# Key-on-partition scores of a causal attention: where the two mask products of a half stand among its score products

## The reference

```python
x = x + attn_a(layernorm(x)); x = x + ffn(layernorm(x))
x = x + attn_b(layernorm(x)); x = x + ffn(layernorm(x))
# attn_a:
S = einsum('hid,hjd->hij', K, Q) * HEAD_DIM ** -0.5
S = where(delta < 0, -inf, S) + decay       # delta = i - j, decay = -|delta|
attn = einsum('hij,hjd->hid', softmax(S), V) @ o_w.T + o_b
# attn_b: scores = q k / sqrt(16), where(causal, scores, -inf), softmax, times v, @ Wo + bo
# ffn: two shared experts, and 32 routed ones of which each token takes 6
```

## Time and profile before

| | |
|---|---|
| median of 3 runs | 3063.31 us (3061.61 to 3063.41) |
| span of the profiled execution | 3108.0 us |
| PE busy in that span | 2643.3 us (85%) |
| DVE / ACT / POOL busy | 2095.1 / 1642.7 / 1403.2 us |
| stretches of attention | about 153 to 846 us and 1700 to 2384 us |
| products at L1607 / masks at L1611 | 1536 / 1024 |

### The profile page before, as it was taken

How to read it: one execution, slowest core, us unless ns; L and a number is a source line. 1 busy time by engine, 2 the same in 40 slices (tenths; PEclk the granted TensorE clock), 3 DMA queues, 4 the chain that set the end, 5 groups by cost and what they waited for, 6 DMA issues and landing times.

```text
span 3108.0 us, 72648 instructions
## 1 busy us (share of the span) xinstructions
PE 2643.3 (85%) x17832; PEld 1963.1 (63%) x17832; DVE 2095.1 (67%) x4682; ACT 1642.7 (53%) x2863; POOL 1403.2 (45%) x1048
## 2 busy tenths in 40 slices
PE   7799999998966799999478999999898759999992
PEld 5555565555555688888465555555555548888882
DVE  8666676675553678888496666766765527787873
ACT  3255443444412688888432554434444118888882
POOL 3420002214155588888655100032232547888885
PEclk9899999999978899999788999999999879999996
DMA  5876545456567689888759643464474668888888
GB/s 205 210 149 124 129 95 125 118 117 176 160 222 221 128 153 156 153 155 155 146 187 221 127 77 74 94 153 107 119 205 157 229 191 150 156 153 154 153 152 204
DMA packets 292685, 478.75 MB, mean 154 GB/s; under 512 B 55702, under 2 KB 200472, under 8 KB 287176
## 3 DMA queue, kind: packets, MB, share of 16 engines
q1 hardware_dynamic: 198992, 341.60, 41.4%
q0 software_dynamic: 92160, 130.08, 25.7%
q10 hardware_dynamic: 1320, 4.46, 0.9%
HBM read 256.33 MB, written 248.91 MB: 163 GB/s over the span
## 4 chain that ended last, share of the span: by engine, by line
PE 49%; issue 18%; DMA 10%; DVE 9%; POOL 6%; DVEq 3%; POOLq 2%; ACT 1%; SPq 1%; another core or an unknown queue 0%; ACTq 0%; PEldq 0%; PEld 0%
PE ps L1593 11%; PE ps L1607 10%; PE ps L1625 9%; DMA expert_sum<-x,route_u 5%; PE ps L1878 4%; DMA expert_rows<-x 3%; PE ps L1896 3%; POOL expert_rows L1481 3%; PE ps L1611 2%; PE ps L1597 2%; DVE split L1167 2%; PE ps L1670 2%; DVEq L1148 1%; POOLq L376 1%; POOL split L1431 1%
## 5 line engine op out<-in xcount | busy, mean ns | idle before, releaser
L1298 ACT ACTIVATE work<-ps 128x1024 f32<-128x1024 f32 (+3 forms) x768 | 595.4, 809 | 691.4 <-PE ps L1611 441.5
L1481 POOL DMA_INDIRECT expert_rows<-x x372 | 364.8, 981 | 1277.6 <-DVE x L975 615.4
L1508 POOL DMA_INDIRECT expert_sum<-x,route_u x512 | 826.5, 1614 | 197.0 <-issue 92.7
L813 DVE TENSOR_REDUCE small<-ps 128x1 f32<-128x512 f32 (+3 forms) x1216 | 728.8, 656 | 185.3 <-PE ps L1597 105.4
L1593 PE MATMUL ps<-split 128*128 128x512 f32 (+3 forms) x1536 | 512.7, 409 | 53.0 <-DVE work L841 37.6
L1607 PE MATMUL ps<-split 128*128 128x512 f32 (+3 forms) x1536 | 501.4, 406 | 20.2 <-DMA split<-split 16.2
L1878 PE MATMUL ps<-split 128*88 128x256 f32 x3072 | 416.6, 285 | 83.9 <-DVE split L1167 50.1
L1878 PEld LDWEIGHTS ps<-split 128*88 128x88 f32 x3072 | 362.7, 155 | 134.8 <-issue 134.0
L1593 PEld LDWEIGHTS ps<-split 128*128 128x128 f32 x1536 | 276.2, 200 | 251.0 <-DVE small L813 139.7
L1896 PE MATMUL ps<-split 97*128 97x256 f32 x3072 | 409.1, 283 | 3.0 <-DVE split L1182 2.8
L1896 PEld LDWEIGHTS ps<-split 97*128 97x128 f32 x3072 | 384.6, 189 | 3.8 <-issue 3.5
(11 more groups left out here) (178 smaller groups left out, 3159.8 us busy)
## 6 DMA issues: line engine op xcount, KB each, us to landing
x<-expert_rows SPq DMA_DIRECT2D x256, 320.0 KB
split<-qks_scratch SPq DMA_DIRECT2D x180, 256.0 KB
qks_scratch<-split SPq DMA_DIRECT2D x64, 512.0 KB, 4.8
expert_rows<-in_pads SPq DMA_DIRECT2D x65, 320.0 KB, 15.3
xT_scratch<-split SPq DMA_DIRECT2D x16, 1024.0 KB
split<-xT_scratch SPq DMA_DIRECT2D x16, 1024.0 KB
split<-w_scratch SPq DMA_DIRECT2D x6, 1792.0 KB
v_scratch<-work SPq DMA_DIRECT2D x64, 136.0 KB, 4.0
```

The source lines that it names most:

```text
L813: v.tensor_reduce(cols[:, heads[0]:heads[0] + len(heads), i], ps[:, task_bank(n), 0:w * len(heads)].rearrange("p (h k) -> p h k", k=w), AX ...
L1298: c.activation(pexp[:, (s % 2) * 2 + h, :, BLK - w:], ps[:, 2 * h:2 * h + 2, BLK - w:], ACT.Exp).then_inc(s_pe, 1)
L1481: pool.indirect_dma_start(rows, bass.IndirectOffsetOnAxis(ap=posu[b][:, t * 8 + k:t * 8 + k + 1], axis=0), row_tile(b, t // TPB, t % TPB), ...
L1508: pool.indirect_dma_start(acc[r], bass.IndirectOffsetOnAxis(ap=idx[:, j, k:k + 1], axis=0), ye[:, r3, k, :], None, compute_op=ALU.add).the ...
```

## The change

In `scores`, the two mask products of a diagonal half move behind both score products. Before, PE ran head 0's product, head 0's mask, head 1's product, head 1's mask. Now it runs both products and then both masks. The operands, the banks, the number of instructions and the semaphores stay as they are; slots without a mask stay as they are too.

```diff
                         last = mm(ps[:, h, BLK - w:], stack[:, r, 1, h, kb * P:kb * P + P],
                                   stack[:, r, 0, h, (qt + 1) * BLK - w:(qt + 1) * BLK],
                                   start=True, stop=kb < 4 * qt, skip_group_check=True)
-                        if kb >= 4 * qt:
-                            last = mm(ps[:, h, BLK - w:BLK - w + P], identb[:, :], maskk[:, :], start=False, stop=True,
-                                      skip_group_check=True)
+                    if kb >= 4 * qt:
+                        for e in range(2):
+                            last = mm(ps[:, 2 * half + e, BLK - w:BLK - w + P], identb[:, :], maskk[:, :], start=False,
+                                      stop=True, skip_group_check=True)
                     last.then_inc(s_st, 1)
```

## The result

The changed kernel takes 3031.49 us (median of 4 runs, 3026.64 to 3032.32) against 3063.36 before. The ratio is 0.9886 with a 95% interval of 0.9864 to 0.9908, that is 28 to 42 us saved, 35 in the middle. The difference of the medians is 32 us. The forecast was 3037, a saving of 26.

What follows compares the result with a forecast made beforehand. PE's time was taken to bound the attention. Reordering the diagonal halves was to save 30.7 us, less 4.9 lost ahead of waits, rounded to 26: from 3063.3 to 3037 us, range 3028 to 3050.

Steps and rivals of the forecast that it cites:

- The bound: Whole kernel: PE, busy 85% of the span, sets the attention, so PE time saved there mostly shortens the kernel.
- p: Diagonal halves: second score product directly behind the first costs 0.23, 0.18, 0.115, 0.11 us at widths 512, 384, 256, 128.
- m: Diagonal halves: second mask directly behind the first costs 0.055 us, with bounds 0.053 and 0.123.
- Rival A: Diagonal halves: second mask's load half uncovered, mask about 0.08 us; 15 us saved, 3048; chance 0.08.
- rival C: Diagonal halves: load time independent of type, second mask 0.11 us; 2.6 us saved, 3061, no measurable change; chance 0.08.
- The sum: All diagonal halves, 128 of each of four widths: PE saves 30.7 us before losses at waits.
- The loss ahead of waits: PE's waits for DVE's output division (L841): 0.35 us saved lost at each of 14, 4.9 us.
- Rival B: Slots 1 to 3: PE's saving turns into waits for free job banks, 10.6 us; 15 us saved, 3048; chance 0.08.
- Rival D: Diagonal halves: second mask's load does not overlap the first mask, mask 0.152 us; 19 us slower, 3082; chance 0.04.

Runs made afterwards that it cites:

- the second profile of before: The kernel before, unchanged, run and profiled again: 3061.44 us (10 runs), ratio 0.9995; its profiled execution spanned 3078.5 us.

## Why the prediction was right

*The bound.* Right. PE sets the attention, and in the units at full clock all of what it saves shortens the unit. In the others the granted clock differs from one execution to the next, and no run separates its part.

*p, a product behind a product.* Right. Taking from the pairs above the part that stands behind a mask leaves about 0.23 us at 512, 0.18 at 384, 0.12 at 256 and 0.11 at 128. The 384 value, which had no row, came out as estimated.

*m, a mask behind a mask.* Right: 0.13 less 0.07, and four in 0.24, give 0.055 to 0.06. Rival A (0.08) and rival C (0.11) don't hold. C is what happens when the masks are fp32r: their m is about 0.11, and the time is 3061.91 where C's was 3061. The Trainium skill, "TensorE: Matmul & The Clock Gate", section "Weight-path perf modes — Fast Weight Load (FWL) and DoubleRow", says that 128 weights that are not FP32 are loaded fast. The traces agree, with 99 ns (101 in the kernel after) against 198 for the same identity in the two types. The Trainium skill's figure of 81 ns for a sustained pair of load and 128-column matmul (same page, section "Back-to-back issue gap"), weighed in the prediction, does not hold for these masks: the second takes 55 to 60 ns.

*The sum.* Per unit 0.92 us instead of the 0.96 forecast: 0.48 of 0.48 in the slots without jobs, 0.45 of 0.48 in the rest. For 32 units that is 29.4 us instead of 30.7. The 2 to 3 us by which the medians differ more are not shown to come from the change.

*The loss ahead of waits.* This is the mis-sized term. I took off 4.9 us, because PE's savings just ahead of a wait for DVE's division would be lost there, and said that those waits would grow by 0.35 us each. They measured 17.9 us in 5 pieces, against 18.8 in 7 before. The five are the long ones (2.53 to 4.57 us), and each is as long as before to 0.02 us; the two that are gone were of 0.43 and 0.44. The chain that ended last of the kernel after shows why, at the end of a unit with a merge:

```profile
341.20 0.66 PE ps L1607 x2
341.86 0.13 PE ps L1612 x2
341.99 0.52 PE ps L1607 x2
342.51 0.13 PE ps L1612 x2
342.64 1.80 PE ps L1671 x8
344.44 0.02 issue
344.46 0.70 DVE x L857
...
345.53 2.38 DVE x L869 x7
```

DVE's work ahead of the division is released by PE's own merge product (L1671), which stands behind the next unit's diagonal slot 0. When PE is earlier, DVE is earlier, and the wait moves with them. Without this term the forecast would have been 3032.6, beside the measured medians of 3031.49 and 3032.72; with it, 26 us lies just under the interval of the ratio.

*Rival B.* DVE took nothing back from the change itself: the 29.31 us stretch of job slots shortened, and PE's waits for L813 are 4.5 us in 14 pieces of at most 0.3, just as in the second profile of before. The prediction's 3.7 us "in all" were only those ahead of max jobs; the first profile had another 3.5 us ahead of L1635. *Rival D* would need a second mask of 0.115 us or more.

## What to carry to other kernels

A matmul shorter than the load of the operand behind it (here 128 columns, 0.053 us, before an fp32r load) leaves that load uncovered, so the price of a short matmul depends on what comes next: gather short matmuls whose own loads are quick, and let long ones stand before long loads. Before a saving is written off against a wait, follow the wait back to what releases it; if that is the engine that got faster, nothing is lost. Where single executions scatter by 1%, read mechanisms from the repeated, undisturbed stretches (here a unit's period) and sizes from the timed runs, and look at the granted clock before a missing gain is put down to another engine.

## What was not expected of the hardware

Doubling the columns of 768 masks, 41 us of streaming, left the time at 0.9973 (0.9951 to 0.9995) of before: about 1.1 of the 1.28 us that a unit's masks stream more went into time in which PE had stood behind uncovered loads. The output products (32 columns of weights) show no such loss behind masks: eight of them at 512 columns take 1.00 us behind products and 0.99 to 1.00 behind masks. And the kernel before spread from 3048 to 3074 us over 25 runs on one chip, while its units without routing kept 37.3 us in both profiles.
